# A graph network on one core: the two attention rounds keep edges on partitions and take the softmax of 16 tiles at once

## The chip, the core and the metric

One core of a Trainium2 chip runs the whole program in one launch. The metric is the device time of that launch in microseconds (us), lower is better. The engines are TensorE (PE, with its weight loads as PEld), VectorE (DVE), ScalarE (ACT), GpSimd (POOL) and SyncE (SP), which here only issues DMAs.

## The reference

A graph of 3125 nodes with 64 features and 103125 edges sorted by destination goes through seven rounds of message passing: one normalised sum, two attention layers, one relational sum, three maxima over edges. The two attention rounds are what the change touches:

```
q = x @ wq + bq;  k = x @ wk + bk;  v = x @ wv + bv;  e = edge_attr @ we
ke = k[src] + e
score = sum(q[dst] * ke, -1) / sqrt(64)
a = exp(score - segment_max(score, dst)[dst])
alpha = a / segment_sum(a, dst)[dst]
out = segment_sum(alpha[:, None] * (v[src] + e), dst) + x @ ws + bs
```

Both kernels fold the weights: per edge they need only the source row x[src] (64 numbers), the 32 attributes and a constant 1, together KA = 97 numbers, and per destination a query of 97 numbers. The weighted sum over edges is taken of the 97 numbers, and the last of them gives the sum of the weights.

## The kernel before, in words

Edges are cut into 808 tiles of P = 128; a chunk is TC = 4 tiles, EC = 512 edges, and there are C = 202 chunks. Each engine has its own program; for every round the helper `chunks` (line 291) writes out its steps. Its arguments are pairs of a lag and a body: at step t an engine runs, in the order in which the pairs stand, each body on chunk t minus its lag. The first steps and the last are written out, the middle is a loop. An engine executes its stream strictly in this order. Engines meet in semaphores alone: `wait` (line 264) blocks the whole engine until each named count is reached, and `c - V + 1` in such a wait says that the buffer of two chunks ago must be free (V = 2 buffers, U = 4 buffers).

In all rounds POOL gathers the source rows: four indirect DMAs per chunk (line 799), each 128 rows of 256 bytes. The sum round (round 0) and the relational round (round 3) turn the rows on PE (line 948, features on partitions), scan them on DVE (line 1095, a running sum that starts again at each new node), turn the states back (line 995), copy them (line 864) and store them (line 891). After the last chunk POOL fetches the state of each node's last edge (line 809), and the node phase computes the next tables.

In an attention round (rounds 1 and 2) features stay on partitions, 97 rows of 512 edges. PE turns the rows (948), builds each edge's query from a window of 128 nodes' queries and a one-hot matrix (973, 12 matmuls) and sums products over features with a matmul by a matrix of 1/8 (981), which puts the same score in all 97 rows. ACT copies the turned rows (878), makes penalties from the flags (856) and takes two exponentials (870, 872). DVE has seven passes of 97 x 512 for a chunk: the product (1129), a running maximum by scan (1152), three differences (1156, 1159, 1161), the weighting (1134) and the decayed sum by scan (1095), and a copy of one column in every second chunk (1149). SP fetches for each chunk flags, one-hots, four windows and the attributes, which lie with features on partitions (716 to 727). The lags are: PE (0, turn), (0, query), (1, score), (3, back); DVE (0, product), (2, accumulate), (1, maxima).

Of the kernel before, what the change touches and what calls it, by code (L numbers as in the profile page):

```python
# [26 lines left out]
P = 128  # L27
TC = 4
EC = TC * P
C = -(-E // EC)  # L30
C += C % 2
CH = C // 2
# [6 lines left out]
TB = -(-T // P)  # L39
GB = 4  # L40
# [9 lines left out]
def gnn_kernel(nc, src, typ, wgt, dst_row, dst_prev, dst_tile, first, edge_t, x, W, out):  # L50
# [15 lines left out]
    onehots = dram("onehots", (C, P, EC), u8)  # L66
    flags = dram("flags", (C, EC), u8)
# [3 lines left out]
    with ctx:  # L71
# [72 lines left out]
        rows = sb("rows", [P, U, 2 * TC * D])  # L144
        sel = sb("sel", [P, U, 3 * EC], f8)
        win = sb("win", [P, U, 2 * TC * 3 * D], bf16)
        dst_b = sb("dst_b", [P, 2 * U, EC], i32)
        tile_same = sb("tile_same", [P, TB, P], f8)
        xe = sb("xe", [P, U, EC])
        near = xe[0:D, :, :].rearrange("p u e -> p (u e)")[:, 0:U * EC // 2].bitcast(f8)\  # L150
            .rearrange("p (u e) -> p u e", u=2 * U)
        prod = sb("prod", [KA, V, EC])
# [4 lines left out]
        runmax = sb("runmax", [KA, 1 + V * EC])  # L157
        diff = sb("diff", [KA, V, EC])
        decay = sb("decay", [KA, V, EC])
        msg = sb("msg", [KA, V, EC])  # L160
# [6 lines left out]
        TURNED, QUERY, SCORE, BACK = range(4)  # L167

# [10 lines left out]
        flags_stored = sem("flags_stored")  # L179
        out_stored = sem("out_stored")  # L180
# [30 lines left out]
        class Round:  # L211

            def __init__(self, r, kind):
# [17 lines left out]
                if kind in (MAX, ATT):  # L231
                    self.pen_ready = shared("pen_ready", C_)
                if kind == MAX:
                    self.relu_ready = shared("relu_ready", C_)
                    self.lifted = shared("lifted", C_)
                if kind == ATT:
                    self.xe_ready = shared("xe_ready", C_)
                    self.query_ready = shared("query_ready", C_)
                    self.prod_ready = shared("prod_ready", C_)
                    self.score_ready = shared("score_ready", C_)  # L240
                    self.carry_ready = shared("carry_ready", -(-C_ // V))
                    self.max_ready = shared("max_ready", C_)
                    self.diff_ready = shared("diff_ready", C_)
                    self.before_ready = shared("before_ready", C_)
                    self.ddecay_ready = shared("ddecay_ready", C_)
                    self.exp_ready = shared("exp_ready", C_)
                    self.decay_ready = shared("decay_ready", C_)
                    self.msg_ready = shared("msg_ready", C_)

                self.rows_ready = [sem(f"rows_ready_{r}_{s_}") for s_ in range(U)]  # L250
# [974 lines left out]
```

## Time and profile before

| | us |
|---|---|
| median of 3 runs (8401.58 to 8409.89) | 8402.46 |
| the profiled execution, its own time | 8402.05 |
| its span | 8400.2 |
| PE busy | 4720.2 (56%) |
| PEld busy | 2797.9 (33%) |
| DVE busy | 3677.3 (44%) |
| ACT busy | 2039.9 (24%) |
| POOL busy | 5613.3 (67%) |

Busy shares over the span mix seven rounds with different limits. The page's line for DVE in 40 slices reads 9 in the two stretches of the attention rounds and 1 in the last half; the line for POOL stays at 6 and 7 but for the node phases. So the table above names no bottleneck; each round has to be read from its own stretch.

### The profile page before, as it was taken

The numbers are of one execution on the slowest core, as the hardware profiler recorded it, in microseconds if no ns is written. First come the engines' busy times: TensorE is split into PE (matmuls) and PEld (weight loads), VectorE is DVE, ScalarE is ACT, GpSimd is POOL, SyncE is SP. The second block draws the span as 40 slices with busy tenths as digits, with TensorE's granted clock in tenths as the row PEclk, the third lists the DMA queues.
The fourth block names the chain that finished last, engine by engine and source line by source line (L and its number), as shares of the span: only waits on it lengthen the run. The fifth ranks groups of instructions, "written<-read, shape, count | busy, mean of one in ns | idle before, by whom it ended". The sixth has DMA issues, their size and how long they took to land.

```text
span 8400.2 us, 120802 instructions
## 1 busy us (share of the span) xinstructions
PE 4720.2 (56%) x23315; PEld 2797.9 (33%) x23315; DVE 3677.3 (44%) x5268; ACT 2039.9 (24%) x4886; POOL 5613.3 (67%) x5874
## 2 busy tenths in 40 slices
PE   2333347777766777776533333666646666566664
PEld 1222234444444444444222222333323333233332
DVE  5444459999967999994133332111111111111112
ACT  1111124444433444442111111111111111111111
POOL 6777756666645666662477775777767777677776
PEclk9999985555555555555555555555556656556555
DMA  4444446665645666662322223444434444444443
GB/s 127 121 127 122 124 92 129 129 130 129 130 96 115 130 130 130 130 130 45 95 59 59 59 59 74 112 112 112 112 88 112 112 112 112 89 108 112 112 112 86
DMA packets 1878056, 896.47 MB, mean 107 GB/s; under 512 B 1293716, under 2 KB 1754724, under 8 KB 1871588
## 3 DMA queue, kind: packets, MB, share of 16 engines
q1 hardware_dynamic: 769476, 429.40, 20.4%
q10 hardware_dynamic: 921120, 272.38, 14.1%
q0 software_dynamic: 187392, 193.93, 12.9%
q8 instruction: 25, 0.41, 0.0%
q14 instruction: 43, 0.35, 0.0%
HBM read 642.32 MB, written 252.51 MB: 107 GB/s over the span
## 4 chain that ended last, share of the span: by engine, by line
PE 23%; issue 18%; POOL 8%; DMA 3%; DVE 2%; ACT 1%; POOLq 0%; DVEq 0%; ACTq 0%
POOL rows L799 8%; PE ps L987 6%; PE ps L962 6%; PE ps L958 5%; DMA rows<-src_table,idx 2%; PE ps L995 2%; PE ps L512 1%; PE ps L563 1%; PE ps L948 1%; PE ps L505 0%; DVE rows L1113 0%; POOL agg L809 0%; DMA agg<-states_sum,last_i 0%; DMA states_sum<-hb 0%; DVE agg L618 0%
## 5 line engine op out<-in xcount | busy, mean ns | idle before, releaser
L799 POOL DMA_INDIRECT rows<-src_table,idx x5656 | 5411.7, 957 | 2553.3 <-issue 1590.2
L948 PE MATMUL ps<-ident,rows 128*64 128x128 f32 x3232 | 839.1, 414 | 1432.3 <-DVE rows L1113 672.6
L1095 DVE TENSOR_TENSOR_SCAN st<-pen,st,ps 128x512 f32<-128x512 f32 x300 | 383.8, 1279 | 2592.3 <-PE ps L987 2592.2
L958 PE MATMUL ps<-ident,rows 128*128 128x128 f32 x1212 | 563.0, 464 | 1173.8 <-issue 1025.6
L995 PEld LDWEIGHTS ps<-ident,st 64*128 64x128 f32 (+2 forms) x4444 | 689.5, 211 | 1269.6 <-issue 1226.5
L995 PE MATMUL ps<-ident,st 64*128 64x64 f32 (+2 forms) x4444 | 905.7, 355 | 242.1 <-issue 216.3
L948 PEld LDWEIGHTS ps<-ident,rows 128*64 128x64 f32 x3232 | 478.4, 164 | 1570.3 <-issue 1394.1
L981 PE MATMUL ps<-prod,eighth 97*97 97x512 f32 x808 | 681.9, 940 | 453.3 <-issue 430.5
L1095 DVE TENSOR_TENSOR_SCAN st<-xe,st,ps 64x512 f32<-64x512 fp8e4 x402 | 511.1, 1271 | 876.2 <-issue 457.7
L958 PEld LDWEIGHTS ps<-ident,rows 128*128 128x128 f32 x1212 | 219.2, 181 | 1430.2 <-issue 1268.4
L882 ACT ACTIVATE xe<-ps,b 128x512 f32<-128x512 f32 x303 | 208.2, 687 | 1916.9 <-PE ps L962 1916.9
L962 PE MATMUL ps<-sel,win 128*64 128x128 fp8e4 x7272 | 647.6, 313 | 0.0
L987 PE MATMUL ps<-xe,w 128*128 128x512 f32 x606 | 625.3, 1135 | 0.0
L856 ACT ACTIVATE pen<-sel 97x512 f32<-97x512 fp8e4 x404 | 254.4, 630 | 1474.1 <-DVE decay L1159 1474.1
L973 PEld LDWEIGHTS ps<-sel,win 128*97 128x97 bf16 x4848 | 586.3, 203 | 17.0
L973 PE MATMUL ps<-sel,win 128*97 128x128 fp8e4 x4848 | 586.4, 309 | 0.0
L1095 DVE TENSOR_TENSOR_SCAN st<-decay,st,msg 97x512 f32<-97x512 f32 x402 | 516.4, 1285 | 132.6 <-DVE msg L1134 131.7
L864 ACT ACTIVATE hb<-ps 128x256 f32<-128x256 f32 (+1 forms) x808 | 346.1, 428 | 762.8 <-PE ps L995 762.7
L1152 DVE TENSOR_TENSOR_SCAN runmax<-pen,runmax,ps 97x512 f32<-97x512 f32 x404 | 512.4, 1268 | 20.2 <-issue 2.2
L962 PEld LDWEIGHTS ps<-sel,win 128*64 128x64 bf16 x7272 | 357.3, 152 | 267.6 <-issue 263.5
L981 PEld LDWEIGHTS ps<-prod,eighth 97*97 97x97 f32 x808 | 142.1, 230 | 520.4 <-issue 505.5
L862 ACT ACTIVATE hb<-ps 128x512 f32<-128x512 f32 x303 | 180.9, 597 | 552.7 <-PE ps L995 520.8
(150 smaller groups left out, 4061.8 us busy)
## 6 DMA issues: line engine op xcount, KB each, us to landing
states_sum<-hb ACTq DMA_DIRECT2D x1010, 128.0 KB
win<-dst_table SPq DMA_DIRECT2D x1616, 72.8 KB
rows<-src_table,idx POOLq DMA_INDIRECT x5656, 2.4
states_att<-hb ACTq DMA_DIRECT2D x404, 194.0 KB
win<-dst_table ACTq DMA_DIRECT2D x1212, 48.0 KB
win<-dst_table SPq DMA_DIRECT2D x1212, 48.0 KB
dst_b<-in_dst_row SPq DMA_DIRECT2D x50, 1024.0 KB
sel<-onehots SPq DMA_DIRECT2D x303, 128.0 KB
```

Source lines behind the costliest of these rows:

```text
L799: pool.indirect_dma_start(rows[:, s, j * D:(j + 1) * D], None, srcs[q.r], bass.IndirectOffsetOnAxis(ap=idx[:, s, j:j + 1], axis=0))\
L856: nc.scalar.activation(pen[0:kw, s % V, :], sel[0:kw, s, EC:2 * EC], ACT.Copy, scale=BIG, bias=-BIG)\
L864: nc.scalar.activation(hb[:, s, 0:TC * kw], bank(BACK, s)[:, 0:TC * kw], ACT.Copy)\
L948: last = nc.tensor.matmul(bank(TURNED, s)[0:D, j * P:(j + 1) * P], rows[:, s, j * D:(j + 1) * D], ident[:, :], is_transpose=True, start=Tr ...
L958: nc.tensor.matmul(bank(TURNED, s)[:, at_j], rows[:, s, j * P:(j + 1) * P], ident[:, :], is_transpose=True, start=True, stop=False)
L962: last = nc.tensor.matmul(bank(TURNED, s)[h * D:h * D + D, at_j], win_pair(s, j, h)[:, i * D:(i + 1) * D], sel[:, s, h * EC + j * P:h * EC ...
L973: last = nc.tensor.matmul(bank(QUERY, s)[0:KA, j * P:(j + 1) * P], win_att(s, j)[:, i * KA:(i + 1) * KA], sel[:, s, j * P:(j + 1) * P], st ...
L981: nc.tensor.matmul(bank(SCORE, s)[0:KA, :], eighth[0:KA, 0:KA], prod[:, s % V, :], start=True, stop=True).then_inc(q.score_ready.sem, 1)
L987: nc.tensor.matmul(bank(QUERY, s), w2[:, q.r - 4, :], xe[:, s, :], start=True, stop=True).then_inc(q.lifted.sem, 1)
L995: last = nc.tensor.matmul(bank(BACK, s)[:, j * w:(j + 1) * w], st[0:w, s % V, j * P:(j + 1) * P], ident[0:w, 0:w], is_transpose=True, star ...
L1095: nc.vector.tensor_tensor_scan(st[0:w, s % V, :], d0, d1, init, op0, op1).then_inc(q.st_ready.sem, 1)
L1152: nc.vector.tensor_tensor_scan(m, pen[0:KA, s % V, :], bank(SCORE, s)[0:KA, :], before[:, 0:1], ALU.add, ALU.max).then_inc(q.max_ready.sem, 1)
```

## The change

In an attention round the edges now stay on partitions, as the gather brings them: a tile is 128 edges by 97 columns in `xe_a`, a ring of UA = 8 chunks instead of 4. POOL gathers straight into it. The attributes go beside the rows: during the sum round SP loads them, PE turns them (`turn_edges`), ACT copies them (`edges_back`) and SP stores them as rows of 128 bytes in `edge_rows`; each attention chunk fetches 4 x 128 of these rows.

PE makes the queries with edges on partitions (12 matmuls, operands swapped); DVE multiplies (128 x 388) and sums over columns to 4 scores for each partition. After GC = 4 chunks, a group of GT = 16 tiles, the scores are turned to 16 x 128 and the softmax's maximum is taken at once: two scans along a tile (`segments`), the tiles' first and last columns turned to one row of 16 (`turn_ends`), a scan over the tiles and three small operations (`running`), turned back (`turn_run`), two operations (`differences`), exponential on ACT, turned back (`turn_weights`). ACT then multiplies the rows by their weights, four instructions per chunk (`weigh`), and makes the decay from flags (`decays`). PE turns the weighted rows, and DVE runs the one scan of 97 x 512 that is left. The score matmul, the running maximum in 97 rows, three differences, the weighting on DVE, the two exponentials of 97 x 512, and the copy of turned rows are gone. Ahead of round 0 DVE makes the penalties of all tiles once, and SP stores them (`pens`).

The core of the diff:

```diff
+                def product(c, s, n):
+                    wait(dve, (q.query_ready, c + 1), (q.rows_ready[s], 16 * TC * (n + 1)), (q.edge_ready[s], 16 * (n + 1)),
+                         (q.scored, c))
+                    nc.vector.tensor_tensor(prod[:, :], bank(TURNED, s)[:, 0:TC * KA], xe_a[:, s, :], ALU.mult)\
                         .then_inc(q.prod_ready.sem, 1)
+                    wait(dve, (q.prod_ready, c + 1))
+                    nc.vector.reduce_sum(score[:, s // GC, o:o + TC], prod[:, :].rearrange("p (j f) -> p j f", f=KA), ...
...
                 def accumulate(c, s, n):
-                    nc.vector.tensor_tensor(msg[:, s % V, :], diff[:, s % V, :], xe[0:KA, s, :], ALU.mult)\
-                    scan(c, s, decay[:, s % V, :], msg[:, s % V, :], ALU.mult, ALU.add)
+                    wait(dve, (q.turned, c + 1), (q.decay_ready, 2 * (c + 1)))
+                    scan(c, s, decay[:, s % V, :], bank(QUERY, s)[0:KA, :], ALU.mult, ALU.add)
...
+                def gather_att(c, s, n):
+                    wait(pool, *sources_stored(q), (q.idx_ready, c + 1), (q.weighted, c - UA + 1))
+                    for j in range(TC):
+                        pool.indirect_dma_start(xe_a[:, s, j * KA:j * KA + D], None, srcs[q.r], ...
...
+                    wait(sp, (q.weighted, c - UA + 1))
+                    sp.dma_start(xe_a[:, s, :].rearrange("p (j f) -> p j f", f=KA)[:, :, D:D + DE],
+                                 edge_rows[cols(c, EC), :].rearrange("(j p) f -> p j f", p=P))\
...
+                def weigh(c, s, n):
+                    wait(act, (q.weight_out, n * NS + gs_ + 1), (q.turned, c - V + 1))
+                    for j in range(TC):
+                        last = nc.scalar.activation(weighted[:, s % V, j * KA:(j + 1) * KA],
+                                                    xe_a[:, s, j * KA:(j + 1) * KA], ACT.Copy,
+                                                    scale=weight[:, gs_, o + j:o + j + 1])
...
+                def turn_weights(c, s, n):
+                    wait(pe, (q.weight_ready, g + 1), (q.kept_out, g + 1))
+                    nc.tensor.matmul(weight_ps[:, 0:m], weight_t[0:m, :], ident[0:m, 0:m],
+                                     is_transpose=True, start=True, stop=True).then_inc(q.weight_turned.sem, 1)
...
-                    chunks(pe, q.steps, (0, turn), (0, query), (1, score), (3, back))
+                    chunks(pe, q.steps, (1, turn_scores), (2, turn_run), (2, turn_weights), (0, query), (1, turn_ends),
+                           (LW, turn_weighted), (LW + 1, back), ring=UA)
...
-                    chunks(dve, q.steps, (0, product), (2, accumulate), (1, maxima))
+                    chunks(dve, q.steps, (2, differences), (0, product), (1, segments), (LW + 1, accumulate),
+                           (1, running), ring=UA)
...
-                    chunks(act, q.steps, (U, features), (0, indices), (U, penalty), (U + 2, exponentials),
-                           (U + 3, states_out), (U + 4, store_states))
+                    chunks(act, q.steps, (B + 2, kept), (B + 2, weights), (B + LW, weigh), (B + LW, decays), (0, indices_att),
+                           (B + LW + 2, states_out), (B + LW + 3, store_states), ring=UA)
```

LW is 5 and B is 4. The bodies of a group (`turn_scores`, `segments`, `turn_ends`, `running`, `turn_run`, `differences`, `kept`, `weights`, `turn_weights`) run in one step of four.

TensorE's stream in the loop of an attention round, before. L948 turns the rows, L973 is the query, L981 the score, L995 the states back; the L275 rows are the registers of waits.

```order
L948 MATMUL ps<-ident,rows 64x128 x4
L275 REGISTER_ALU
L973 MATMUL ps<-sel,win 97x128 x12
L275 ISA
L981 MATMUL ps<-prod,eighth 97x512
L275 ISA
L995 MATMUL ps<-ident,st 128x97 x4
```

Here `back` (L995) turns the scan of two steps earlier than DVE's newest one. The same place now, at the end of a group; L1148 is the query, L1168 `turn_ends`, L1197 `turn_weighted`, L1213 `back`, L1178 and L1181 `turn_run`, L1190 `turn_weights`.

```order
L1148 MATMUL ps<-win_sb,sel 128x97 x12
L338 REGISTER_ALU
L1168 MATMUL ps<-ident,seg_max 1x16 x2
L338 REGISTER_ALU
L1197 MATMUL ps<-ident,weighted 97x128 x4
L338 REGISTER_ALU
L1213 MATMUL ps<-ident,st 128x97 x4
L338 REGISTER_ALU
L1178 MATMUL ps<-ident,run_in 16x1
L1181 MATMUL ps<-kept_row,ones_row 97x16
L1190 MATMUL ps<-ident,weight_t 128x16
L1148 MATMUL ps<-win_sb,sel 128x97 x12
```

The score matmul has gone, the turn stands behind the query, and the next chunk's query stands behind both `back` and, once in four steps, the turns of the group's weights.

VectorE's stream in the same loop, before. L1129 is the product, L1134 the weighting, L1095 the summing scan, L1152 the maximum's scan.

```order
L1129 TENSOR_TENSOR prod<-ps,xe 97x512
L1134 TENSOR_TENSOR msg<-diff,xe 97x512
L275 ISA
L1095 SCALAR_TENSOR_TENSOR st<-decay,st,msg 97x512
L275 REGISTER_ALU
L1152 SCALAR_TENSOR_TENSOR runmax<-pen,runmax,ps 97x512
L275 REGISTER_ALU
L1156 TENSOR_TENSOR diff<-ps,runmax 97x512
L1159 TENSOR_TENSOR decay<-runmax,pen 97x512
L1161 TENSOR_TENSOR decay<-decay,runmax 97x512
```

And now, in the step that closes a group. L1374 and L1378 are the product and its sum, L1387 and L1390 `segments`, L1341 the summing scan, from L1405 on `running`.

```order
L1374 TENSOR_TENSOR prod<-ps,edges_a 128x388
L1378 TENSOR_REDUCE score<-prod 128x4
L338 ISA
L1387 SCALAR_TENSOR_TENSOR tile_max<-pens_sb,ps 16x128
L1390 SCALAR_TENSOR_TENSOR seg_max<-pens_sb,tile_max 16x128
L338 ISA
L1341 SCALAR_TENSOR_TENSOR st<-decay,st,ps 97x512
L338 REGISTER_ALU
L1405 SCALAR_TENSOR_TENSOR run<-row_pens,run,ps 1x16
```

The summing scan stands behind the product of the same step, and it works on the chunk six before it, which is the chunk that PE's `back` of that step turns.

## Rows read from the trace of the kernel before

**Rows 1.** Busy time by stage: sum, attention, relational, maxima rounds; PEclk 1.00 is 2.4 GHz

```profile
core 0: us, PE busy (x) PEld busy (x) DVE busy (x) ACT busy (x) POOL busy (x), PEclk, DMA share, GB/s
64.00:1075.00 1011.00, 331.33 (x1604) 207.84 (x1604) 413.73 (x1009) 157.20 (x596) 765.12 (x808) 1.00 0.46 123
1200.00:2350.00 1150.00, 836.49 (x3980) 540.48 (x3977) 1041.94 (x1354) 475.51 (x1081) 719.73 (x733) 0.59 0.61 130
...
4200.00:5000.00 800.00, 264.09 (x1280) 165.76 (x1280) 271.20 (x320) 94.08 (x319) 605.25 (x640) 0.50 0.29 59
5300.00:6150.00 850.00, 533.58 (x2896) 276.66 (x2892) 108.73 (x85) 161.64 (x341) 642.62 (x681) 0.59 0.50 112
```

**Rows 2.** Instruction groups in 1300:2300: busy us, mean ns, idle before and releaser

```profile
L799 POOL DMA_INDIRECT rows<-src_table,idx x629 | 618.9, 984 | 382.7 <-ACT idx L845 222.4 <-issue 160.3
...
L1152 DVE TENSOR_TENSOR_SCAN runmax<-pen,runmax,ps 97x512 f32<-97x512 f32 x157 | 199.2, 1269 | 7.2
...
L856 ACT ACTIVATE pen<-sel 97x512 f32<-97x512 fp8e4 x157 | 98.9, 630 | 586.1 <-DVE decay L1159 586.1
...
L864 ACT ACTIVATE hb<-ps 128x388 f32<-128x388 f32 x157 | 74.2, 472 | 0.0
```

**Rows 3.** Timeline, ends of rounds 0 to 2 on POOL: start us, duration us

```profile
63.51 0.94 POOL L799 DMA_INDIRECT rows<-src_table,idx  x1 [15.54 <-DMA src_table<-zn]
...
1074.59 0.94 POOL L799 DMA_INDIRECT rows<-src_table,idx  x1 [0.30 <-issue]
...
1157.94 0.94 POOL L799 DMA_INDIRECT rows<-src_table,idx  x1 [41.57 <-ACT idx L845]
...
2420.80 0.94 POOL L799 DMA_INDIRECT rows<-src_table,idx  x1 [0.30 <-issue]
...
2460.50 0.94 ACTq L891 DMA_DIRECT2D states_att<-hb  x2
2465.65 0.94 POOL L809 DMA_INDIRECT agg<-states_att,last_i  x1 [43.91 <-DMA states_att<-hb]
...
2556.10 0.94 POOL L799 DMA_INDIRECT rows<-src_table,idx  x1 [59.55 <-ACT idx L845]
...
3860.98 0.94 POOL L809 DMA_INDIRECT agg<-states_att,last_i  x1 [44.00 <-DMA states_att<-hb]
```

**Rows 4.** Timeline of PE in attention: two pieces at 2.4 GHz, three at 1.2 GHz

```profile
1180.44 0.83 PE L973 MATMUL ps<-sel,win 128*97 128x128 fp8e4 x12
...
1182.02 0.55 PE L995 MATMUL ps<-ident,st 97*128 97x97 f32 x4
...
2430.00 0.91 PE L995 MATMUL ps<-ident,st 97*128 97x97 f32 x4 [0.30 <-DVE st L1095]
...
2430.70 1.06 PE L948 MATMUL ps<-ident,rows 128*64 128x128 f32 x4
...
2431.55 1.49 PE L973 MATMUL ps<-sel,win 128*97 128x128 fp8e4 x12
```

**Rows 5.** Groups of the node phases in 200:3700, sizes near the new ones

```profile
L386 DVE TENSOR_TENSOR split_r<-ps,split 128x388 f32<-128x388 f32 x12 | 6.7, 561 | 90.4 <-ACT split L375 90.4
...
L377 ACT ACTIVATE split<-split_r 128x97 bf16<-128x97 f32 x2 | 0.6, 285 | 0.8 <-DVE split_r L386 0.8
```

**Rows 6.** Timeline of the start: small operations, and the first one-hots

```profile
31.02 0.29 PE L927 MATMUL ps<-ident,wq 65*64 65x65 f32 x1 [31.02 <-DMA w<-in_W]
...
54.03 0.29 DVE L1035 TENSOR_REDUCE within<-agg 128x1 f32<-128x128 f32 x1
...
55.72 0.18 DVE L1076 TENSOR_TENSOR deg<-edges_le,ps 128x25 f32<-128x25 f32 x1 [0.78 <-PE ps L936]
...
66.89 0.87 DVE L1102 TENSOR_SCALAR sel<-dst_b,nodes 128x128 fp8e4<-128x128 int32 x4 [8.24 <-DMA xe<-flags]
```

**Rows 7.** DMA queues in 1300:2300: packets, MB, share of 16 engines

```profile
q1 hardware_dynamic: 143106, 77.68, 35.2%
q0 software_dynamic: 20074, 20.59, 13.2%
```

More of the change, by code:

```diff
@@ L39 @@
 TB = -(-T // P)
+UA = 2 * 4
+GC = UA // 2
+GT = GC * TC
+NG = -(-C // GC)
+NS = 2
+LW = GC + 1
+B = 4
+PF = 2 * P + 1
 GB = 4
@@ L316, in batch, with group, near_att @@
             return s // U, m, slice(c, c + m) if isinstance(c, int) else bass.ds(c, m)
+        def group(c, s, n):
+            if s % GC != GC - 1 and not (isinstance(c, int) and c == C - 1):
+                return None
+            return n * NS + s // GC, s // GC, (s % GC + 1) * TC
+        def near_att(v, h):
+            return sel[0:KA, v, (1 + h) * EC:(2 + h) * EC]
         def cols(c, k=1):
@@ L937, in _ @@
                 .then_inc(pe_pre, 1)
+            pe.wait_ge(rows_set, 1)
+            for b in range(TB):
+                w = min(P, T - b * P)
+                last = nc.tensor.matmul(last_ids[:, b * P:b * P + w], tile_last[0:w, b:b + 1], ident[0:w, 0:w],
+                                        is_transpose=True, start=True, stop=True)
+            last.then_inc(ids_turned, 1)
             for q in rounds:
@@ new lines, in turn_ends @@
+                def turn_ends(c, s, n):
+                    if not group(c, s, n):
+                        return
+                    g, gs_, m = group(c, s, n)
+                    wait(pe, (q.seg_ready, g + 1), (q.run_ready, 4 * g))
+                    for o, e in ((first_ps, 0), (last_ps, P - 1)):
+                        last = nc.tensor.matmul(o[:, 0:m], seg_max[0:m, e:e + 1], ident[0:m, 0:m],
+                                                is_transpose=True, start=True, stop=True)
+                    last.then_inc(q.ends_turned.sem, 1)
@@ new lines, in turn_weights, with turn_weighted @@
+                def turn_weights(c, s, n):
+                    if not group(c, s, n):
+                        return
+                    g, gs_, m = group(c, s, n)
+                    wait(pe, (q.weight_ready, g + 1), (q.kept_out, g + 1))
+                    nc.tensor.matmul(weight_ps[:, 0:m], weight_t[0:m, :], ident[0:m, 0:m],
+                                     is_transpose=True, start=True, stop=True).then_inc(q.weight_turned.sem, 1)
+                def turn_weighted(c, s, n):
+                    wait(pe, (q.weighted, c + 1), (q.st_ready, c - V + 1))
+                    for j in range(TC):
+                        last = nc.tensor.matmul(bank(QUERY, s)[0:KA, j * P:(j + 1) * P],
+                                                weighted[:, s % V, j * KA:(j + 1) * KA], ident[:, :],
+                                                is_transpose=True, start=True, stop=True)
+                    last.then_inc(q.turned.sem, 1)
@@ L1004, in _ @@
                 else:
-                    chunks(pe, q.steps, (0, turn), (1, back))
+                    chunks(pe, q.steps, *[(0, turn_edges)] * (k == SUM), (0, turn), (1, back))
                 if k == MAX:
```

403 lines of the change are left out of this document (293 added, 110 removed).

## The prediction

> **What bounds the kernel now.** I read the busy times by stage first, because an average over seven rounds says nothing. In the sum, relational and maxima rounds [rows 1] POOL is the one engine that never pauses but for its own issue gap: 807 gathers from 63.51 to 1074.59 us are 1.253 us each, 5.01 us for a chunk of four [rows 3]. The reader should see that this pace is the same while the other engines and the DMA share differ widely. In the attention rounds it is not: DVE is busy 1041.94 of 1150 us, 91%, and POOL only 63% [rows 1]. 157 chunks per 1000 us make 6.37 us for a chunk [rows 2]. The groups say who waits for whom: POOL loses 222 us waiting for indices, and ACT, which writes them, loses 586 us waiting for a difference of DVE [rows 2]. So DVE sets the end there, with seven passes over 97 x 512, and the rest follows. Round 1 takes 1307.7 us from its first gather (1157.94) to the fetch of last states (2465.65), round 2 1304.9 us (2556.10 to 3860.98) [rows 3]. These 2612.6 us are what the change can touch to any extent; the other rounds keep their gathers.
>
> **What the new attention chunk costs, engine by engine.** Two limits are simple. POOL: four gathers, 5.01 us, as in the sum round. DVE: product 128 x 388 is 0.56 us, the like of L386 [rows 5]; its sum over columns reads the same 388 elements, 0.56 us (at 128 elements a reduction takes 0.29 us [rows 6], so both follow the element count); the summing scan is 1.27 us [rows 2]. For a group add two scans of 128 columns (between 0.29, an operation of 128 elements, and 0.5; I take 0.4), four small operations at 0.18 and two of 128 columns at 0.29 [rows 6]: 2.1 us, 0.5 per chunk. DVE is 2.9 us of work against 5.8 before. ACT: four weightings at 0.285 [rows 5], the decay 0.63 like L856, the copy of states 0.47 [rows 2], and some 0.5 of small ones: 2.75 us. Neither engine binds by its sum. SP issues 6.5 DMAs per chunk for 7; its fetch of attributes now waits, like the gather, for `weighted` eight chunks back, and the next chunk's windows are queued behind that wait, still seven chunks ahead of their use.
>
> **The step as a circle.** What the sums leave out is the order of two streams. In a step PE does `query`, `turn_weighted`, `back`; DVE does `product`, its sum, the scan. DVE's product waits for PE's query of this step, the scan stands behind the product, `back` waits for that scan, and the next query stands behind `back`. Before, `back` turned a scan that DVE had made a step earlier, so the circle was open; now the lag of `accumulate` and of `back` are both LW + 1. Around it at 1.2 GHz: from the start of `back` to the next matmul 0.70 us (2430.00 to 2430.70), query 1.49 [rows 4], product 0.56, sum 0.56, scan 1.27, and some 0.12 for four handovers: 4.7 us. `turn_weighted` lies beside the DVE part and costs nothing while that is 2.4 us long (4 turns, 1.06 [rows 4]).
>
> Once in four steps the group is closed. `turn_scores` stands before the query (0.25, near the 0.29 of a small transpose [rows 6]), and the two scans of `segments` stand between sum and summing scan (0.8): 1.05 us. In the next step PE reaches the query only behind `turn_run` and `turn_weights`: 0.25 for the turn, 0.29 and 0.29 on DVE, 0.28 for the exponential (L377's size [rows 5]), 0.2 for the turn back, 0.2 for handovers: 1.5 us in which PE stands and DVE has no product. `running` itself hides behind `back`. Four steps: 4 x 4.7 + 1.05 + 1.5 = 21.35 us, 5.34 per chunk, over POOL's 5.01.
>
> **The clock moves this.** At 2.4 GHz the query is 0.83 and `back` 0.55 against 0.91 [rows 4]: 0.94 us less per step, with the small turns 4.1 us less per group, 4.3 per chunk. Then POOL binds. The granted clock before was 0.59 in attention with PE 73% busy, that is 18% of the time at 2.4 GHz, and the new streams have similar runs of work (back, query and turn together) and pauses, so I keep 18%: 0.74 us per group, 20.6 us, 5.15 per chunk. The old loop also held 0.6 us a chunk that is not busy time of its bounding engine (6.37 against 1041.94 us for some 181 chunks, 5.77); part of that is one known wait, and I add 0.1 for the rest: **5.25 us**. Bounds: 5.01 (POOL) and 5.5 (no fast stretch, and twice the additions).
>
> The trace has PE's clock at 1.00 in the sum round and at 0.50 in the relational round with the same 33% busy [rows 1], so the busy share does not decide it. The Trainium skill (TensorE: Matmul & The Clock Gate, What's actually happening) says that the default is the throttled state and that activity releases it. By that the denser stream of `back`, query and turn could hold 2.4 GHz, and the time would be that of the first rival below; the sum round's row at 1.00 with little activity does not agree with it.
>
> **Does the ring of 8 chunks hold?** Gather c waits until chunk c - 8 is weighted. The first chunk of a group is weighted about 4 us after its closing step's scan, and the rows for the product four steps on are needed about 14 us after that; gathering them takes 5.0 and landing some 2.5. So POOL is let go 6 us early. At this cover the gather is no part of the circle; if the softmax chain grew by over 6 us, each further us would cost a quarter us per chunk.
>
> **Round total.** To the first product: four gathers 5.0, landing and query, 9 us. 201 steps of 5.25: 1055. After the last product comes the last group's softmax (some 8 us), four chunks at ACT's 2.5 us, turn, scan, back and copy (3.9), and 5.15 us from the last store's issue to POOL's fetch (2460.50 to 2465.65 [rows 3]), less overlap: 25 us, where before 43.9 us lay behind the last gather. Sum 1089 us. Saved: 1307.7 - 1089 and 1304.9 - 1089, together 434.6 us.
>
> **Other rounds.** In the sum round each chunk gets a load, four small turns, a copy and a store. DMA is at 0.46 of 5.01 us there [rows 1], PE at 33%, ACT at 16%, and POOL waits for none of them: nothing, with the cover of the gathers; up to 5 us for a longer tail. At the start DVE makes penalties: about sixteen operations, by sizes 10 us, before the one-hots that began at 66.89 [rows 6]. The gathers fill four buffers meanwhile (20 us from 63.51), so only a rest shows: 3 us taken, 0 to 12 as bounds. No operation of the change shortens these rounds.
>
> Sum, against the profiled execution's 8402.05 us (the median of the runs, 8402.46, is the same within 0.01%): 8402.05 - 434.6 + 3 = **7970 us**.
>
> **Rivals.**
>
> *POOL's pace binds.* The circle stays under 5.01 us because PE gets more of 2.4 GHz, or handovers are shorter. For it: the sum is over POOL's pace by 5%, less than its own uncertainty. Against: 1.5 us of standing per group is certain in the order. A round is then 1012 for gathers and 26 of drain, 1038: 8402.05 - 536.6 + 3 = 7868 us.
>
> *The attribute rows crowd the DMA engines.* A chunk now takes 512 pieces of 128 bytes instead of 32 of 2 KB. DMA share before is 0.61 of 6.37 us, 3.9 us. Queue q1 spends 39 ns per packet (35.2% of 16 engines over 1000 us, 143106 packets [rows 7]). Flags for 128 partitions (0.31) and the old attributes (about 0.2) go, flags for 97 (0.24) come: 3.6 us without attributes. 512 pieces at 39 ns are 1.25 us, together 4.9 of 5.25: full, but not binding. At 66 ns, between the two queues' prices, it is 5.7, with queues forming 5.8 per chunk: rounds of 1200 us, 8190 us. For it: the engines would be over 85% busy. Against: 128 bytes should cost less than the 580 of a window's piece.
>
> The skill (DMA: Bandwidth & Descriptors, Specifications) gives 512 bytes as the least transfer for line rate, below which the engine reads, modifies and writes; that speaks against the change, and no row here has a piece of 128 bytes.
>
> *Slower than before, by the same pieces.* The gather queue q0 spends 105 ns per packet (13.2%, 20074 packets [rows 7]). If an attribute piece costs that, 3.36 + 3.6 = 6.96 us per chunk, rounds of 9 + 1399 + 25 = 1433 us, 8402.05 + 253 + 3 = 8658 us. It decides from 85 ns a piece, where a round equals the old 1306 us. Against it: a q0 packet is 1 KB.
>
> **How the numbers follow.** The circle at 5.05 to 5.5 us: 0.55, 7910 to 8070 us. POOL's pace: 0.24. Crowded DMA, still faster: 0.15. Slower by the pieces or by a ring that doesn't hold: 0.05. About 0.01 for a cancellation. A difference under 0.2% (17 us) could not be told from none. The range for 8 in 10 takes POOL's case in below and half of the crowded case above: 7855 to 8130. Faster 0.94, same 0.01, slower 0.05.
>
> **What would show it.** Right: in attention POOL pauses once per group for `weighted`, PE stands before the query behind `turn_weights` about 1.5 us, `back` waits for the scan of the same step in every step, DVE is under 60% busy, gathers per chunk 5.1 to 5.5 us, clock 0.55 to 0.65. Wrong: gathers 1.25 us apart throughout (POOL's pace), or DVE's product waiting for attributes with the DMA share over 0.9 (crowding), or a sum round longer than 1030 us.

## The result: 8439.86 us, 0.4% slower, and where it stands in the profile after

| | before | after |
|---|---|---|
| median us (runs) | 8402.90 (8401.58 to 8409.89, 5) | 8439.86 (8434.05 to 8449.23, 5) |
| ratio after / before | | 1.0043, 95% interval 1.0029 to 1.0058 |
| the profiled execution | 8402.05 | 8434.05 |
| round 1, first gather to fetch of last states | 1307.7 | 1312.7 |
| round 2, the same | 1304.9 | 1329.2 |

7970 us were predicted, with a range from 7855 to 8130. The time did not fall; it rose by 37 us. The two attention rounds, which should have given back 435 us, took 29 us more; the sum round took 4.7 us more (1026.3 for 1021.6), the others moved by about 1 us each. That round 2 took 16 us more than round 1 stays open; the long issues found below account for 3.5 us of it. The stages after, in the windows of [rows 1] for the sum and attention rounds, and in windows moved by 100 us for the other two:

```profile
core 0: us, PE busy (x) PEld busy (x) DVE busy (x) ACT busy (x) POOL busy (x), PEclk, DMA share, GB/s
64.00:1075.00 1011.00, 441.17 (x2400) 307.21 (x2400) 418.03 (x1007) 195.24 (x796) 765.97 (x805) 1.00 0.61 150
1200.00:2350.00 1150.00, 570.09 (x3908) 476.50 (x3908) 507.96 (x920) 483.44 (x1671) 682.42 (x724) 0.50 0.63 127
4300.00:5100.00 800.00, 264.07 (x1280) 165.72 (x1280) 271.48 (x321) 93.92 (x320) 604.99 (x641) 0.50 0.29 59
5400.00:6250.00 850.00, 524.23 (x2829) 273.80 (x2829) 113.10 (x100) 160.70 (x336) 629.87 (x668) 0.60 0.47 107
```

In attention DVE fell from 91% busy to 44%, PE from 73% to 50%, POOL from 63% to 59%, and the DMA share stayed (0.63 for 0.61). Every computing engine is at or below 59%: none of those in this row sets the pace by its own work. DVE's new operations cost what was predicted (groups in 1300:2300, as [rows 2]):

```profile
L913 POOL DMA_INDIRECT edges_a<-src_table,idx x624 | 588.8, 944 | 412.1 <-ACT weighted L1022 233.1 <-issue 167.4 <-ACT idx L987 11.6
L1341 DVE TENSOR_TENSOR_SCAN st<-decay,st,ps 97x512 f32<-97x512 f32 x156 | 198.6, 1273 | 0.0
L1022 ACT ACTIVATE weighted<-edges_a,weight 128x97 f32<-128x97 f32 x624 | 183.2, 365 | 35.7 <-ACT hb L976 27.4 <-issue 4.5
L1148 PE MATMUL ps<-win_sb,sel 128*128 128x97 bf16 x1872 | 182.3, 282 | 140.5 <-DMA win_sb<-dst_table 140.5
L1374 DVE TENSOR_TENSOR prod<-ps,edges_a 128x388 f32<-128x388 f32 x157 | 88.2, 562 | 522.1 <-PE ps L1148 511.8 <-issue 10.3
L1378 DVE TENSOR_REDUCE score<-prod 128x4 f32<-128x388 f32 x156 | 86.8, 557 | 16.2
```

Product 562 ns and its sum 557 (0.56 foretold for each), scan 1273. On ACT the four weightings of a chunk take 1.18 us for 1.14. 156 chunks are 39 groups in 1000 us: 25.6 us for a group, 6.4 for a chunk, and not 5.25. That this is so near the old kernel's 6.37 is a coincidence: another engine sets it now. The last column of the L1148 row names a wait that the prediction did not have: the query waits for its windows, `win_sb<-dst_table`. The waits in the same stretch (us in total, times, longest) show that this happens once per group, 39 times and 3.6 us each on average, and that DVE and POOL lose more time beside it:

```profile
DVE prod L1374 <- PE ps L1148: 511.8, 152, 8.6
...
POOL edges_a L913 <- ACT weighted L1022: 233.1, 60, 7.1
...
PE ps L1148 <- DMA win_sb<-dst_table: 140.5, 39, 4.1
```

The windows are fetched by SP. This is SP's queue over one group, with the waits of PE and DVE beside it (start us, duration us):

```profile
1744.59 0.29 SPq L804 DMA_DIRECT2D sel<-flags  x1
1745.19 9.06 SPq L816 DMA_DIRECT2D sel<-onehots  x1
...
1755.02 1.88 SPq L822 DMA_DIRECT2D win_sb<-dst_table  x4
1757.28 0.38 SPq L824 DMA_DIRECT2D edges_a<-edge_rows  x1
1758.07 0.34 SPq L816 DMA_DIRECT2D sel<-onehots  x1
1759.01 1.88 SPq L822 DMA_DIRECT2D win_sb<-dst_table  x4
...
1760.38 1.14 PE L1148 MATMUL ps<-win_sb,sel 128*128 128x97 bf16 x12 [3.62 <-DMA win_sb<-dst_table]
1761.22 0.38 SPq L824 DMA_DIRECT2D edges_a<-edge_rows  x1
1761.62 0.56 DVE L1374 TENSOR_TENSOR prod<-ps,edges_a 128x388 f32<-128x388 f32 x1 [6.84 <-PE ps L1148]
...
1765.65 0.34 SPq L814 DMA_DIRECT2D pens_sb<-pens  x1
...
1770.05 0.29 SPq L804 DMA_DIRECT2D sel<-flags  x1
1770.57 9.17 SPq L816 DMA_DIRECT2D sel<-onehots  x1
```

An issue of one-hots takes 0.34 us, but the one behind the group's fetch of near flags (L804) takes 9.06 and 9.17. From one L804 to the next lie 25.46 us, and SP has no idle time in them that a semaphore ends (the view of its own waits is empty for 1300:2300): four chunks at about 3.8 us (with register work between the issues), the long issue at 9.1, and 0.6 each for the fetches of penalties and of flags. SyncE, which the table of busy times does not even list, sets the pace. The page's chain of what ended last says the same in one row, where in the kernel before SP does not appear:

```profile
SPq L816 10%; POOL edges_a L906 8%; PE ps L1205 6%; PE ps L1136 6%; SPq L822 6%; PE ps L1132 5%; PE ps L1213 4%; DMA edges_a<-src_table,idx 3%; PE ps L1122 3%; DMA sel<-flags 2%; PE ps L584 2%; SPq L824 2%; SPq L818 2%; PE ps L1113 1%; DMA win_sb<-dst_table 1%
```

What is new in the fetch of flags is its shape. Before, one DMA a chunk put 512 flags on 128 partitions. Now one DMA a group puts four chunks' flags on 97: 388 pieces of 512 bytes. The theory (A) that the experiments test: 97 is a prime number, all 388 pieces go to one DMA engine's queue, and the next issue is held until that queue has room. The Trainium skill (DMA: Bandwidth & Descriptors, "Why a DMA increments its semaphore by 16 and not by 1", on how many engines) has the first half: a transfer is spread over the largest number of engines up to 16 that divides the slowest dimension of both of its sides, so 96 or 128 partitions use 16 and 127 use one. The trace agrees: the fetch to 97 partitions gets, beside a semaphore update 0.43 us after its issue, a single one at 13.8 us (medians); with 128 partitions, below, sixteen updates come from 3.4 to 6.0 us.

### The profile page after: what moved, and what is told of

It reads as the page before. It is cut to its first block, busy times and chain, and to the rows that moved or that the text cites. A ratio compares the mean times of both kernels' runs of the same rounds, so it can differ in the third digit from the quotient of the medians.

```text
span 8432.2 us, 123362 instructions
## 1 busy us (share of the span) xinstructions
PE 4261.9 (51%) x24036; PEld 2772.4 (33%) x24036; DVE 2506.4 (30%) x4334; ACT 2090.8 (25%) x6406; POOL 5548.3 (66%) x5874
## 3 DMA queue, kind: packets, MB, share of 16 engines
q1 hardware_dynamic: 1064928, 451.96, 21.9%
## 4 chain that ended last, share of the span: by engine, by line
PE 30%; issue 29%; SPq 21%; POOL 9%; DMA 7%; DVE 3%; ACT 1%; ACTq 0%; POOLq 0%; DVEq 0%
SPq L816 10%; POOL edges_a L906 8%; PE ps L1205 6%; PE ps L1136 6%; SPq L822 6%; PE ps L1132 5%; PE ps L1213 4%; DMA edges_a<-src_table,idx 3%; PE ps L1122 3%; DMA sel<-flags 2%; PE ps L584 2%; SPq L824 2%; SPq L818 2%; PE ps L1113 1%; DMA win_sb<-dst_table 1%
## 5 line engine op out<-in xcount | busy, mean ns | idle before, releaser
L906 POOL DMA_INDIRECT edges_a<-src_table,idx x4040 | 3821.9, 946 | 1519.0 <-issue 1167.8
L913 POOL DMA_INDIRECT edges_a<-src_table,idx x1616 | 1525.0, 944 | 1133.0 <-ACT weighted L1022 567.8
L1213 PE MATMUL ps<-ident,st 64*128 64x64 f32 (+2 forms) x4444 | 926.5, 361 | 495.8 <-issue 462.9
L1132 PE MATMUL ps<-ident,edges_a 128*128 128x128 f32 x1212 | 563.0, 465 | 1172.4 <-issue 1024.6
L1341 DVE TENSOR_TENSOR_SCAN st<-pen,st,ps 128x512 f32<-128x512 f32 x300 | 383.9, 1280 | 2591.9 <-PE ps L1205 2591.7
L1213 PEld LDWEIGHTS ps<-ident,st 64*128 64x128 f32 (+2 forms) x4444 | 705.3, 215 | 1109.5 <-issue 1064.9
L1341 DVE TENSOR_TENSOR_SCAN st<-edges_a,st,ps 64x512 f32<-64x512 fp8e4 x402 | 511.3, 1272 | 874.0 <-issue 475.8
L1148 PE MATMUL ps<-win_sb,sel 128*128 128x97 bf16 x4848 | 472.1, 282 | 406.9 <-DMA win_sb<-dst_table 406.9
L1136 PE MATMUL ps<-sel,win_sb 128*64 128x128 fp8e4 x7272 | 647.3, 313 | 0.0
L1374 DVE TENSOR_TENSOR prod<-ps,edges_a 128x388 f32<-128x388 f32 x404 | 226.9, 562 | 1360.0 <-PE ps L1148 1279.8
L1205 PE MATMUL ps<-edges_a,w 128*128 128x512 f32 x606 | 625.8, 1136 | 0.0
L1148 PEld LDWEIGHTS ps<-win_sb,sel 128*128 128x128 fp8e4 x4848 | 425.5, 143 | 433.2 <-issue 357.3
L1341 DVE TENSOR_TENSOR_SCAN st<-decay,st,ps 97x512 f32<-97x512 f32 x402 | 511.6, 1273 | 8.9 <-PE ps L1197 8.7
L1022 ACT ACTIVATE weighted<-edges_a,weight 128x97 f32<-128x97 f32 x1616 | 474.4, 365 | 82.7 <-ACT hb L976 64.8
L1197 PE MATMUL ps<-ident,weighted 128*97 128x128 f32 x1616 | 460.2, 438 | 5.2 <-ACT weighted L1022 4.5
```

Of the source, the lines that this page charges most:

```text
L906: pool.indirect_dma_start(rows[:, s, j * D:(j + 1) * D], None, srcs[q.r], bass.IndirectOffsetOnAxis(ap=idx[:, s, j:j + 1], axis=0))\
L913: pool.indirect_dma_start(xe_a[:, s, j * KA:j * KA + D], None, srcs[q.r], bass.IndirectOffsetOnAxis(ap=idx_a[:, s, j:j + 1], axis=0))\
L1022: last = nc.scalar.activation(weighted[:, s % V, j * KA:(j + 1) * KA], xe_a[:, s, j * KA:(j + 1) * KA], ACT.Copy, scale=weight[:, gs_, o + ...
L1132: nc.tensor.matmul(bank(TURNED, s)[:, at_j], rows[:, s, j * P:(j + 1) * P], ident[:, :], is_transpose=True, start=True, stop=False)
L1136: last = nc.tensor.matmul(bank(TURNED, s)[h * D:h * D + D, at_j], win_pair(s, j, h)[:, i * D:(i + 1) * D], sel[:, s, h * EC + j * P:h * EC ...
L1148: last = nc.tensor.matmul(bank(TURNED, s)[:, j * KA:(j + 1) * KA], sel[:, v, j * P:(j + 1) * P], win_att(v, j)[:, i * KA:(i + 1) * KA], st ...
```

## The experiments

Each variant changes only how flags are fetched (in one of them also the count that their reader waits for), or the order or lag of TensorE's bodies. Flags on more than 97 partitions write rows that nobody reads.

### First lot: on a chip that was slow for every kernel

Near flags on 128 partitions:

```diff
-                    sp.dma_start(sel[0:KA, 0:m, (1 + gs_) * EC:(2 + gs_) * EC].bitcast(u8),
-                                 flags[of, :].rearrange("(o u) e -> o u e", o=1).to_broadcast([KA, m, EC]))\
+                    sp.dma_start(sel[0:128, 0:m, (1 + gs_) * EC:(2 + gs_) * EC].bitcast(u8),
+                                 flags[of, :].rearrange("(o u) e -> o u e", o=1).to_broadcast([128, m, EC]))\
```

> The changed kernel with one edit: the flags of a group are spread over 128 partitions instead of 97. Theory A (the 97-partition broadcast keeps SP's next DMA issue waiting 9 us once per group, and SP's issue time, 15 us of work and 9 us of standing, is the 25.5 us of a group): the long issue of the one-hots goes, and the circle of query, product, scan and back, or POOL, binds: 20 to 21.5 us per group, 7860 to 8000 us. Theory B (DMA engines crowded by the 128-byte attribute rows): more bytes of flags change nothing or make it worse, 8430 us or over. Theory C (the PE-DVE circle at 1.2 GHz alone gives 25 us): no change, 8430 us.

The same with 102 in place of 128:

> The changed kernel with the flags of a group over 102 partitions: more bytes than 97, but 102 divides by 6 where 97 and 101 are primes. If one DMA engine gets the whole broadcast when the partitions don't divide: the issue behind it stands 1 to 2 us instead of 9, and the time is within 1% of the 128-partition run. If the size of the broadcast makes the stall: 9.5 us as before, 8430 us. If any count that is not a multiple of 16 makes it: 9.5 us as well.

Near flags on 128, and `back` one step later:

```diff
-                           (LW, turn_weighted), (LW + 1, back), ring=UA)
+                           (LW, turn_weighted), (LW + 2, back), ring=UA)
```

> As the flags over 128 partitions, and PE's back one step later (LW + 2), so that it turns a scan of the step before and the circle is open. If the circle binds then: group period from about 21 to 20.0 us (POOL's pace), some 50 to 130 us less than with the flags alone. If POOL already binds there: no change. If something else binds: no change.

Near flags on 128, and the query ahead of the group's turns:

```diff
-                    chunks(pe, q.steps, (1, turn_scores), (2, turn_run), (2, turn_weights), (0, query), (1, turn_ends),
+                    chunks(pe, q.steps, (1, turn_scores), (0, query), (2, turn_run), (2, turn_weights), (1, turn_ends),
```

> As the flags over 128 partitions, and PE's query ahead of turn_run and turn_weights, the circle left closed. If the 1.5 us of standing before the query in the closing step is on the path: about 1.5 us less per group, 100 groups in two rounds, up to 150 us less, until POOL's 20.0 us binds. If not: no change.

Measured: 10460.11, 10441.77 (one run), 10243.94 and 10428.36 us, where the kernel before took 9882.98 (9833.52 to 9942.60, 7 runs) on this chip: ratios 1.058, 1.0358 and 1.0547 for the three timed ones. None of these can be set against its expectation as a time, for rounds that no variant touches are long too: the sum round of the first variant takes 1236.7 us for 1026.3. Its gathers there keep their pace and then stop together with all other computing engines; 46 pauses of over 1.5 us in which no engine works are 111 us of that round:

```profile
611.92 0.95 POOL L906 DMA_INDIRECT edges_a<-src_table,idx  x1 [0.30 <-issue]
616.21 0.94 POOL L906 DMA_INDIRECT edges_a<-src_table,idx  x1 [3.34 <-remote]
```

The reader is to see durations as ever (0.94) and a pause whose releaser the trace puts outside this core. What paused this chip is not known. One thing of this lot stands, since it is no sum of times: no issue of one-hots takes more than 0.76 us with 128 partitions and 1.23 with 102 (a product of 6 and 17), in place of 9 in each group. Where the trace has all semaphore updates of the fetch with 102, six follow the first one, in place of the single one with 97. The three larger questions were put again on other chips.

### Second lot: the same three, beside the unaltered kernel

> The changed kernel, unaltered, run beside its three variants on the same chip, because the first set of variants ran on a chip on which the kernel before itself took 9883 us against 8402 us. Every theory expects 8440 us and a ratio to the kernel before of 1.004 if this chip is like the first one, and one issue of 9 to 10 us on SyncE's queue in every group of four chunks, behind the fetch of the near flags.

Measured: 8460.63 us (8456.28 to 8462.62), the kernel before 8405.48 (8403.49 to 8405.90, 7 runs), ratio 1.0067 (1.0050 to 1.0084). 100 long issues in the two rounds, median 9.26 us. 20 us more than expected, of which the longer issues (937 us together, 920 in the first profile) account for some 17.

> The near flags are spread over 128 partitions instead of 97, nothing else. Theory A (SyncE's issue is the bound, because the issue behind the 97-partition fetch takes 9 us): that issue falls to about 0.4 us, SyncE's queue needs some 16 us a group of four, the group goes from 25.6 us to the closed circle's 3 x 4.5 + 4.7 + closing work = about 19.5 to 21 us, 50 groups in two rounds give 2 x 250 us back: 7920 to 8000 us. Theory B (the stall only covers another wait: the DMA engines are loaded by the 128-byte attribute rows, or the closing step of a group is as long for its own reasons): 8350 to 8450 us, and the windows still come late once a group.

Measured: **8055.66 us** (8053.28 to 8058.77), ratio 0.9585 (0.9569 to 0.9601), 405 us under the unaltered kernel. The median issue of one-hots is 0.35 us, the longest 1.01. PE no longer waits for windows. SP's queue in this kernel, at the same place of a group as above:

```profile
1899.29 0.42 SPq L804 DMA_DIRECT2D sel<-flags  x1
1899.95 0.34 SPq L816 DMA_DIRECT2D sel<-onehots  x1
```

And SP itself now waits once a group, for a result of DVE (1300:2100; us in total, times, longest), so it no longer sets the pace:

```profile
SPq L342 <- DVE ref L1423: 174.9, 37, 5.1
```

Theory A's wait is gone, and the rival's 8350 to 8450 is excluded: there are a third more pieces (512 for 388), and the long issue is gone with 405 us. But 8056 lies 56 us above the 7920 to 8000 that A gave; a group takes 21.9 to 22.1 us, not 19.5 to 21. That rest is taken apart in the next section.

> As the previous one, and TensorE turns the weighted rows back two steps after their weighting rather than one, so that the circle query, product, sum, scan, back no longer passes through the weighting. Theory A with the circle as the next bound: a step falls from 4.5 us to 3 to 4 us (VectorE's 2.9 us of work in a chunk is the floor), POOL's 5.01 us a chunk for four gathers becomes the bound, and the time is 7850 to 7920 us, some 50 us or more under the previous kernel. Rival: the step is held by VectorE and ScalarE taking turns inside one chunk, whatever the place of back: as the previous kernel, within 15 us.

The edit is that of the first lot: `back` now turns the scan of the step before. The weighting, which the expectation names, was no part of the circle.

Measured: **7881.37 us** (7881.07 to 7884.45), ratio 0.9378 (0.9363 to 0.9394), 174 us under the previous one. The three plain steps of a group, product to product, are 3.30, 3.95 and 4.27 us (medians) where they were 4.47, 4.47 and 4.68; a group is 19.8 to 20.4, and POOL, at 5.01 for four gathers, needs 20.0. Its 808 gathers take 1010.0 us in each attention round and 1014.7 in the sum round. The circle was the bound, and opening it gives the pace to POOL.

Both edits of TensorE's bodies together:

> As the previous one, and TensorE takes the query of the next chunk ahead of the turns of the attributes' sums and weights of the chunk before. If the query's place in TensorE's row is part of the circle it gives up to another 0.5 us a chunk where POOL doesn't bound (20 to 50 us in both rounds); if POOL's pace is the bound by then, nothing, within 10 us of the previous kernel.

Measured: 7882.86 us (7882.38 to 7887.36), ratio 0.9381: no difference, as the case "POOL's pace is the bound by then" has it. The order inside the group did change (the closing step is 6.06 and 5.6 us in place of 8.4 and 3.3), and it is worth nothing there.

### Third lot: is it the number of partitions, or that it is prime; and the closing step

```diff
+                    for lo, hi in ((0, KA - 1), (KA - 1, KA)):
+                        sp.dma_start(sel[lo:hi, 0:m, (1 + gs_) * EC:(2 + gs_) * EC].bitcast(u8),
+                                     flags[of, :].rearrange("(o u) e -> o u e", o=1).to_broadcast([hi - lo, m, EC]))\
+                            .then_inc(q.near_ready[gs_].sem, 16)
```

> The changed kernel; the near flags go to the same 97 partitions as before, but by two DMAs, one of 96 partitions and one of the last. That is one more issue (0.3 us) a group and not one byte more. Theory A (97 is prime, so the descriptors of one DMA all go to one engine's ring, and the next issue waits there 9 us): the long issue goes as with 128 partitions, 8050 to 8080 us. Rival (97 rows behave otherwise than 128 because of what shares or leaves out partitions in the tile, such as ScalarE reading the tile while it is written): as the changed kernel, 8440 to 8460 us.

Measured: 8049.13 us (8048.36 to 8061.91), ratio 0.9580 (0.9565 to 0.9595), against 8401.71 for the kernel before (15 runs). The same 97 partitions and bytes, one DMA more, and the time is that of 128 partitions (8056 on another chip):

```profile
1703.47 1.12 SPq L805 DMA_DIRECT2D sel<-flags  x2
1704.91 0.34 SPq L817 DMA_DIRECT2D sel<-onehots  x1
```

So neither the partitions left out nor the amount of data makes the long issue; that all pieces go to one engine, which a prime count of partitions brings about, does.

101 in place of 97, on the changed kernel:

> The changed kernel with the near flags on 101 partitions, also a prime. Theory A: the stall stays and is as long or 4% longer, 9.5 to 10 us a group; 8450 to 8480 us. Rival (what mattered was 97 against a longer transfer): the stall goes, about 8055 us.

Measured: 8505.46 us (one run). The stall stays, 100 times, median 9.69 us for 9.13 and 9.26 with 97:

```profile
1704.31 0.29 SPq L804 DMA_DIRECT2D sel<-flags  x1
1704.91 9.71 SPq L816 DMA_DIRECT2D sel<-onehots  x1
```

101 holds, 102 and 128 do not. The time is 25 us over the expectation's upper end. 404 pieces for 388 make 0.43 to 0.56 us, about 31 ns a piece. The trace's DMA records say where the hold ends. They start one piece in about 35 ns, and when the long issue ends, 275 of the 388 pieces (median) or 291 of the 404 have started. 113 are left in both, and never fewer than 108 or more than 123 in all 300 long issues (both profiles of the changed kernel and this one). The next issue goes through when about 113 pieces are left.

The query ahead of the group's turns, with 128 partitions, again:

> Near flags on 128 partitions, and TensorE takes the next chunk's query ahead of the group's turns of maxima, kept parts and weights. In the closing step of a group the query stood 2.9 us behind the weights of ScalarE (18.69 against 15.75 us in the trace). If these turns are the reason, the product comes up to 2.9 us earlier, but the scan of that step waits for the rows weighted with them, so part comes back: a group of 19.8 to 21 us rather than 22.0, 50 groups in two rounds, 100 to 215 us less than the kernel with 128 partitions: 7840 to 7955 us. Rival: the closing costs what it costs whatever the order, 8045 to 8065 us.

Measured: 7915.71 us (7914.21 to 7917.28), ratio 0.9422 (0.9407 to 0.9436), 140 us under the kernel with 128 partitions alone (133 under the split fetch, which ran on this chip), and a group of 19.9 to 20.9 us. The query's place behind the group's turns cost what the trace said; its last part comes back as expected, for `turn_weighted` now waits.

The kernel before with its flags on 97 partitions:

```diff
-                    sp.dma_start(sel[:, s, EC:2 * EC].bitcast(u8), flags[one(c)].to_broadcast([P, EC]))\
+                    sp.dma_start(sel[0:KA, s, EC:2 * EC].bitcast(u8), flags[one(c)].to_broadcast([KA, EC]))\
```

> The kernel before, with its flags (one DMA a chunk) on 97 partitions instead of 128. Theory A by pieces: 97 pieces on one engine instead of 388 hold the next issue a quarter as long, about 2.3 us, in every chunk; SyncE's queue then needs some 6 us of the 6.37 us of a chunk, so the time stays within 0.2% (8402) though the issue is long. If a stall is a fixed 9 us whatever the pieces, SyncE needs 12.7 us a chunk and the time is about 10900 us. Rival without any ring: no long issue here at all and no change of time.

Measured: 8402.38 us (8399.63 to 8405.21), ratio 1.0002 (0.9993 to 1.0011). The time is as expected and the reason is not: there is no issue of 2.3 us to be hidden. The rival without any long issue was right:

```profile
1504.31 0.28 SPq L716 DMA_DIRECT2D sel<-flags  x1
1504.77 0.39 SPq L718 DMA_DIRECT2D sel<-onehots  x1
1505.94 2.21 SPq L724 DMA_DIRECT2D win<-dst_table  x4
```

0.39 for 0.33, and now and then 2.21 for 1.88 at the windows. These flags too go to one engine: the semaphore that they share with one-hots and windows gets up to 82 updates a chunk where the kernel before has up to 96, that is 2 for 16 from the flags. So a prime count by itself does not hold the queue; it takes many pieces as well. 97 pieces are fewer than the 108 to 123 that are left when a hold ends, so there is nothing to wait for. No run has a count between 97 and 388, and why there is such a limit was not tested.

## Why the prediction was wrong, step by step

**The step that failed** is the sentence on SP: "SP issues 6.5 DMAs per chunk for 7; its fetch of attributes now waits, like the gather, for `weighted` eight chunks back, and the next chunk's windows are queued behind that wait, still seven chunks ahead of their use". It counted the issues and looked for a wait behind them. It took each issue at its usual price, though the fetch of flags was new in shape. The price of the one behind it was 9.1 us, 2.2 us for each chunk, and it made SP's row 6.4 us a chunk, over the circle's and POOL's. Nothing in the kernel before has a DMA of this shape, so no row could price it, and it should have had bounds; it got none, and none of the rivals had SP in it. The rival on DMA engines did count the pieces, at 0.24 us a chunk, but spread over 16 engines. The lead of seven chunks is wrong too: one-hots and windows have U = 4 buffers, and their fetch waits for the query of four chunks before; but a longer lead would not have helped a row that is too long in every group. On the chip on which both were timed the changed kernel took 8461 us, 491 over the prediction; without the long issue it takes 8056, so this step is 405 us of it.

**The rest, about 86 us** (8056 for 7970), is in the attention rounds: 1131.0 and 1131.4 us for 1089. The predicted pieces can be checked in the kernel with 128 partitions, which has no stall. One plain step and the closing of a group:

```profile
1903.67 1.27 DVE L1341 TENSOR_TENSOR_SCAN st<-decay,st,ps 97x512 f32<-97x512 f32 x1
...
1905.04 0.88 PE L1213 MATMUL ps<-ident,st 97*128 97x97 f32 x4 [1.67 <-issue]
...
1905.71 1.19 PE L1148 MATMUL ps<-win_sb,sel 128*128 128x97 bf16 x12
...
1906.99 0.56 DVE L1374 TENSOR_TENSOR prod<-ps,edges_a 128x388 f32<-128x388 f32 x1 [2.06 <-PE ps L1148]
...
1908.13 1.27 DVE L1341 TENSOR_TENSOR_SCAN st<-decay,st,ps 97x512 f32<-97x512 f32 x1
...
1911.67 0.56 DVE L1374 TENSOR_TENSOR prod<-ps,edges_a 128x388 f32<-128x388 f32 x1 [2.27 <-PE ps L1148]
...
1912.81 0.40 DVE L1387 TENSOR_TENSOR_SCAN tile_max<-pens_sb,ps 16x128 f32<-16x128 f32 x1
...
1913.70 1.28 DVE L1341 TENSOR_TENSOR_SCAN st<-decay,st,ps 97x512 f32<-97x512 f32 x1
...
1915.08 0.88 PE L1213 MATMUL ps<-ident,st 97*128 97x97 f32 x4
...
1917.12 0.21 ACT L1001 ACTIVATE kept_row<-run_diff 1x16 f32<-1x16 f32 x1 [0.37 <-ACT hb L976]
1917.44 0.47 PE L1181 MATMUL ps<-kept_row,ones_row 1*97 1x16 f32 x2 [1.38 <-issue]
1918.01 0.18 ACT L1004 ACTIVATE kept_part<-ps 97x16 f32<-97x16 f32 x1 [0.67 <-PE ps L1181]
1918.10 0.31 ACT L1012 ACTIVATE weight_t<-weight_t 16x128 f32<-16x128 f32 x1
1918.50 0.26 PE L1190 MATMUL ps<-ident,weight_t 16*128 16x16 f32 x1 [0.59 <-ACT weight_t L1012]
1918.69 1.16 PE L1148 MATMUL ps<-win_sb,sel 128*128 128x97 bf16 x12
...
1919.95 0.56 DVE L1374 TENSOR_TENSOR prod<-ps,edges_a 128x388 f32<-128x388 f32 x1 [3.08 <-PE ps L1148]
```

- *The circle: right, 0.23 too long.* Scan to back 1.37, back to query 0.67, query to product 1.28, product to the next scan 1.14: 4.46 us, for 4.7. The query takes 1.19 where [rows 4] had 1.49 for the operands the other way round. That the circle is real is shown by the experiment that opens it (174 us).
- *The group's two scans and the turn of scores: right.* The product comes 0.21 us late (4.68 for 4.47) and the scan 0.89 us (13.70 for 1911.67 + 1.14 = 12.81): 1.10 for 1.05.
- *The next query behind the turns: 2.9 us for 1.5.* By the plain step the query would start 0.67 behind `back`, at 15.75; it starts at 18.69. The working had the turn, two operations, the exponential and the turn back. It left out the kept parts: L1001, L1181 and L1004 stand ahead of the exponential in ACT's row and take from 17.12 to 18.10, and L1001 itself stands behind the copy of states. The experiment with the query first gets back 1.2 to 2.0 us of a group's 22.0.
- *The clock: no gain.* The working gave 0.74 us a group for 18% of the time at 2.4 GHz. In this kernel the granted clock reads 1.00 in round 1 and 0.50 in round 2:

```profile
1200.00:2200.00 1000.00, 585.40 (x3955) 484.89 (x3956) 515.85 (x931) 477.42 (x1676) 692.90 (x735) 1.00 0.73 151
2450.00:3430.00 980.00, 574.75 (x3874) 474.52 (x3872) 507.18 (x917) 468.76 (x1648) 675.72 (x717) 0.50 0.72 151
```

The rounds take 1131.0 and 1131.4 us, and `back` is 368 ns at the median in both. The matmuls are as long as the 1.2 GHz ones of [rows 4] (four of `back` in 0.88 us for 0.91), so 1.00 in the record is not what this stream ran at, and the term should have been nothing. In [rows 4] the short pieces (0.55, 0.83) were real, but few: in 1200:2200 of the kernel before 74 of 625 matmuls of `back` are under 0.8 of the median, here none of 728.

The same holds for the row on which the prediction argued that the busy share does not decide the clock. These are the turns of rows (L948) of the kernel before in the sum and the relational round:

```profile
64.00:1075.00 1011.00, 207.92 (x804) 107.89 (x804) 1.00 0.46 123
4200.00:5000.00 800.00, 165.37 (x640) 85.81 (x640) 0.50 0.29 59
```

0.26 us of PE time each in both, and the median of one is 421 ns in both. The sum round's 1.00 thus shows no faster clock, and it neither supports that argument nor contradicts what the prediction quotes from the Trainium skill beside it.

Together: 4 x 4.47 + 0.21 + 0.89 + 2.94 = 21.9 us a group, measured 21.9 to 22.1, against 20.6 + 0.4 (the prediction's 0.1 a chunk for unknown waits) = 21.0. Over 201 steps of 5.50 instead of 5.25 that is 50 us a round; the ends of a round are 8 us shorter than foretold; with both rounds 84.

**The rivals.** POOL's pace did not bind here, but does as soon as `back` stands a step later: that rival's 7868 is within 0.2% of the 7881 of that kernel. The crowded DMA engines, with 0.15 and 0.05, did not happen. Queue q1 in 1300:2300, as [rows 7]:

```profile
q1 hardware_dynamic: 211222, 75.44, 35.6%
```

68000 more packets take the same share: 27.0 ns each for 39, an average over pieces from 4 bytes to 2 KB. The trace's records have the pieces of 128 bytes at 12.9 ns each (mean of 79872), so 512 of them are 6.6 us of engine time a chunk, 0.41 us of 16 engines where the prediction had 1.25. At POOL's pace the DMA share is 0.79 (`back` one step later, 1200:2150), and nothing waits for attributes. The least transfer of 512 bytes for line rate, which the prediction cites from the Trainium skill (DMA: Bandwidth & Descriptors, Specifications), shows in the price: 128 bytes in 12.9 ns are half the rate of 512 bytes in 27 ns (median). It did not show in the time.

**The ring** of eight chunks: POOL has a long wait for `weighted` once a group, as said, up to 7.1 us in the changed kernel because the group is long, 2.4 us with 128 partitions. **The sum round** went to 1026.3 us, within its 5 us; the start cost nothing (first gather at 63.01 for 63.51), where 3 us stood.

## What to carry to other kernels

Before pricing a change, ask of each new or reshaped DMA how its partitions divide: a broadcast of hundreds of pieces to a prime number of partitions goes to one engine and holds the issue behind it, while 96 + 1 or 128 partitions cost no hold. The engine that only issues DMAs has a row of its own to add up, issue by issue, even if no table of busy times lists it. And when a large cut in work moves nothing, look for the one wait that comes once per period: here 3.6 us of PE in 25.6 named the transfer, and its issuer named the cause.

## What the runs showed of the hardware

- The DMA issue behind one of 388 pieces on 97 partitions took 9.13 and 9.26 us at the median of two profiles (100 long issues in each, 8.1 to 12.3), behind 404 on 101 partitions 9.69, behind 512 on 128 partitions 0.35, behind 97 on 97 partitions 0.38 (median). The long fetch itself issued in 0.29: the price stands in the row of the next one.
- The held issue ended when 108 to 123 pieces of the fetch before it had not yet started, in all 300 cases; one engine started a piece in about 35 ns.
- A granted clock of 1.00 and of 0.50 came with equal matmuls and equal rounds (1131.0 and 1131.4 us), and in the kernel before with equal turns (421 ns). Durations, not the recorded level, say what a stream ran at.
- Loads of 128-byte pieces cost 12.9 ns each of an engine's time, 512-byte pieces 27 (median).
- One chip ran the kernel before 18% slower (9883 us) and the variants 30% (10460 for 8056, 10244 for 7881), with pauses of all computing engines at once and gathers as long as ever (0.94 us); there the ratio to the kernel before was 1.058 for the variant that has 0.9585 elsewhere. A ratio is no protection against such a chip; a round that the edit does not touch shows it (1236.7 us for 1026.3).
